# A deformable-convolution stage whose pairs are interpolated three turns ahead of their own, with the residual sums moved to the turn that ends a contraction

## The reference, cut to what matters

```python
x = x + layer0(gn(x))                       # batch 8, 256 channels, 64 x 64
    # qkv = w_qkv @ x; per head a 3x3 neighbourhood attention plus a 3x3 dynamic kernel; w_proj
x = x + modulated_dcn(gn(x), w_off, b_off, w)

def modulated_dcn(x, w_off, b_off, w):
    om = conv3x3(x, w_off) + b_off           # 27 channels: offsets y and x of 9 taps, 9 masks
    off, mask = om[:, :18], sigmoid(om[:, 18:27])
    py, px = base + tap + off                # a fractional place for each pixel and tap
    v = bilinear(x, py, px)                  # 4 neighbours, 4 weights
    return einsum('bckhw,ock->bohw', v * mask, w)
```

## Time and profile before

| | us |
|---|---|
| median of 3 runs | 5197.19 |
| lowest and highest run | 5186.94 and 5206.48 |
| the profiled execution | 5200.59 |
| its span (first to last instruction) | 5198.8 |
| TensorE busy | 4855.1 |
| VectorE busy | 4324.4 |
| ScalarE busy | 2332.2 |
| GpSimd busy | 2257.9 |

### The profile page before, as it was taken

How to read it: one execution, slowest core, us unless ns; L and a number is a source line. 1 busy time by engine, 2 the same in 40 slices (tenths; PEclk the granted TensorE clock), 3 DMA queues, 4 the chain that set the end, 5 groups by cost and what they waited for, 6 DMA issues and landing times. The chain is left out here.

```text
span 5198.8 us, 80271 instructions
## 1 busy us (share of the span) xinstructions
PE 4855.1 (93%) x26864; PEld 2671.2 (51%) x26864; DVE 4324.4 (83%) x11040; ACT 2332.2 (45%) x5584; POOL 2257.9 (43%) x2311
## 2 busy tenths in 40 slices
PE   7889999999999999999999999999999999988888
PEld 4545554555545555455545555455554555544444
DVE  6848888888888888888889888888888888987776
ACT  2244444344453444444444444434444344455555
POOL 0014444444444444444444444444444444455565
PEclk9999999999999999999999999999999999999999
DMA  5447878878787878978789787888878878798888
GB/s 180 143 153 263 284 260 321 284 270 278 274 325 269 275 272 281 339 252 282 266 274 339 261 278 266 288 315 270 281 267 310 290 263 275 258 356 313 328 324 305
DMA packets 490804, 1446.79 MB, mean 278 GB/s; under 512 B 47380, under 2 KB 117404, under 8 KB 490140
## 3 DMA queue, kind: packets, MB, share of 16 engines
q0 software_dynamic: 331776, 1208.11, 66.9%
q1 hardware_dynamic: 158620, 233.55, 12.6%
HBM read 1309.08 MB, written 132.39 MB: 277 GB/s over the span
## 5 line engine op out<-in xcount | busy, mean ns | idle before, releaser
L883 POOL DMA_INDIRECT G<-table,IDX x2304 | 2257.0, 980 | 2902.3 <-DVE V L1566 2094.9
L902 PE MATMUL ps<-VT,s_wconv 128*128 128x512 f32 x4608 | 2273.9, 617 | 102.0 <-ACT VT L1283 37.7
L1566 DVE SCALAR_TENSOR_TENSOR V<-G,WT,V 128x256 f32<-128x256 f32 x4320 | 1892.7, 479 | 115.8 <-DVE V L1566 3.7
L1283 ACT ACTIVATE VT<-ps 128x512 f32<-128x512 f32 x1152 | 686.7, 596 | 2294.5 <-PE ps L1122 1848.3
L902 PEld LDWEIGHTS ps<-VT,s_wconv 128*128 128x128 f32 x4608 | 823.7, 193 | 919.1 <-issue 847.0
L1553 DVE SCALAR_TENSOR_TENSOR V<-G,WT 128x256 f32<-128x256 f32 x2304 | 1009.0, 478 | 244.6 <-ACT G L1269 135.4
L1122 PEld LDWEIGHTS ps<-s_ident,V 128*128 128x128 f32 x4320 | 539.1, 142 | 650.4 <-issue 647.1
L1303 DVE TENSOR_TENSOR E<-ps,s_band 128x512 f32<-128x512 f32 x1024 | 648.7, 682 | 268.9 <-PE ps L964 137.3
L1269 ACT ACTIVATE G<-G,WT 128x256 f32<-128x256 f32 x1872 | 846.4, 498 | 16.1 <-DMA G<-table,IDX 12.3
L1122 PE MATMUL ps<-s_ident,V 128*128 128x128 f32 x4320 | 655.5, 275 | 47.6 <-DVE V L1566 43.0
L940 PE MATMUL ps<-XN,s_wqk 128*128 128x512 f32 x1024 | 488.5, 605 | 19.7 <-ACT XN L1182 16.7
(11 more groups left out here) (109 smaller groups left out, 3008.4 us busy)
## 6 DMA issues: line engine op xcount, KB each, us to landing
table<-E SPq DMA_DIRECT2D x256, 256.0 KB
G<-table,IDX POOLq DMA_INDIRECT x2304
X<-in_x SPq DMA_DIRECT2D x64, 512.0 KB
G<-in_x SPq DMA_DIRECT2D x56, 512.0 KB, 4.3
x<-X SPq DMA_DIRECT2D x56, 512.0 KB, 5.5
R<-x SPq DMA_DIRECT2D x56, 512.0 KB
out<-R SPq DMA_DIRECT2D x56, 512.0 KB
out<-X SPq DMA_DIRECT2D x8, 512.0 KB
```

What stands on the lines that cost most here:

```text
L883: e.indirect_dma_start(G[a % NG][:, :], None, T[b % 2], bass.IndirectOffsetOnAxis(ap=IDX[:, col:col + 1], axis=0)).then_inc(d_g[a % NG], 16)
L902: mm = e.matmul(CV[oh][:, :], s_wconv[:, h, t, oh * P:(oh + 1) * P], VT[U % 2][:, h, :], start=(t == 0 and h == 0), stop=(t == 8 and h == 1))
L1283: e.activation(VT[U % 2][:, :, 2 * P * pair:2 * P * (pair + 1)], BK[banks.place[use]][:, :].rearrange("p (h n) -> p h n", h=2), ACT.Copy). ...
L1566: e.scalar_tensor_tensor(vt[:, :], gt[:, q * C:(q + 1) * C], WT[:, col, q:q + 1], vt[:, :], ALU.mult, ALU.add).then_inc(lerp[q - 1], 1)
```

## The change

The loop that writes the steps is turned round. The lerps of pairs 0, 1 and 2 stand at the start of an image. From then on one round is: lerp m+2, two fills, turn m, the gather of pair m+5, scale m+4. So a lerp stands directly behind the turn whose transposes free its `V` buffers (m-1), and three turns ahead of its own. The two sums of a chunk each stand one turn earlier in the list, in the same step as the contraction that completes `CV`. Instructions, buffers and waits stay the same, but whether a pair is scaled on ScalarE or on VectorE is decided at the place where the scale step is written, which is now two pairs earlier: 203 pairs are scaled on VectorE in place of 216, and 949 on ScalarE in place of 936.

```diff
+        def interpolate(m):
+            if m < PAIRS:
+                steps.append(("lerp", b, m))
+
         steps.append(("gather", b, 0, NG))
         scale(0)
         scale(1)
         done = fill(0, done)
+        interpolate(0)
+        scale(2)
+        interpolate(1)
+        scale(3)
         for m in range(PAIRS):
-            steps.append(("lerp", b, m))
+            interpolate(m + 2)
             done = fill(2 * m + 1, done)
-            steps.append(("turn", b, m - 1))
-            if m > 0:
-                steps.append(("gather", b, 2 * (m - 1) + NG, 2 * m + NG))
-            scale(m + 2)
             done = fill(2 * m + 2, done)
-        steps.append(("turn", b, PAIRS - 1))
+            steps.append(("turn", b, m))
+            steps.append(("gather", b, 2 * m + NG, 2 * m + 2 + NG))
+            scale(m + 4)
         steps.append(("conv.end", b))
...
-                    if t == 1 and pair == 0 and u > 8:
+                    if t == 0 and pair == 1 and u > 8:
                         add_residual(b * NCH + c - 1, 0)
-                    elif t == 1 and pair == 1 and u > 8:
+                    elif t == 1 and pair == 0 and u > 8:
                         add_residual(b * NCH + c - 1, 1)
```

## The result

The changed kernel takes 5403.21 us (median of 4 runs, 5390.26 to 5407.31) against 5193.37 us for the kernel before (4 runs, 5186.94 to 5206.48): a ratio of 1.0396, 95% interval 1.0369 to 1.0424. The forecast of 5140 us, and the range up to 5225, are both wrong: the change makes the kernel slower by 4%.

What follows compares the result with a forecast made beforehand. TensorE, 93% busy, was taken as the bound, with VectorE close behind. From 5200.6 us: -33 lerps, -36 sums, -12 clock, -15 scales, +30 front work, +7 image starts gave 5141.6, written 5140 (ratio 0.989), range 5080 to 5225.

Steps and rivals of the forecast that it cites:

- What it costs: front work behind a lerp: Banded products queued on VectorE behind a lerp make TensorE wait for PSUM banks; +30 us, bounds 0 and 230.
- the slow rival: Half of 116 banded products have no slack, banks come free too late, low clocks follow; 5250 us, chance 0.18.
- an upper bound of 230 us: Added waits for banded products if none of the 116 places where VectorE was early had any slack.
- the slack at place 2: Near 586.76 us: TensorE wants the bank after 4.0 us, VectorE needs 3.3 for lerp and product; 0.7 us to spare.
- waits for ScalarE copies that grow by tens of microseconds: Sign in TensorE's waits, left alone in the sum, that would show the forecast wrong.
- Lerps, -33: Lerps three turns ahead cut the transposes' 43.0 us of waits for them to 10; bounds 0 and -43.
- 10.3 us of allowed lateness: How late VectorE may be at a turn with lerps three rounds ahead, up from 6.5 us.
- Residual sums, -36: Sums one turn earlier take 36 of 39.0 us from contractions' waits for them; bounds 0 and -39.
- the low clock at place 1, -12: Half-clock stretch from 786.7 to 790.1 us goes with the residual wait, 1.7 us in each of seven images.
- Scales and last image, -15: Scales two pairs earlier ease the last image's lerp, gather, scale loop that TensorE waits for; bounds 0 and -55.
- in the middle that gains TensorE nothing: Earlier scales spare VectorE waits for ScalarE, but in the middle gain TensorE nothing beyond the terms already counted.

Runs made afterwards that it cites:

- e17: Changed kernel with each of its two fills one quota step later, so turns stand behind the same front steps as in the kernel before; ratio 1.0231.
- e10: Kernel before with nine `G` buffers in place of ten and one place less for the statistics' loads; ratio 1.0013.
- e7: Kernel before with four `V` buffers in place of six, every instruction at its old place; ratio 1.0143.
- e13: Kernel before with only the fills half a round later against turns and lerps, lead and room of lerps kept at 1.5 rounds; ratio 1.0166.
- e1: Kernel before with the two residual sums alone moved one turn earlier; ratio 1.0033.
- e2: Changed kernel with the two residual sums back at their old turns; ratio 1.0457 to the kernel before.
- e3: Changed kernel with each lerp two turns ahead of its own instead of three; ratio 1.0169 to the kernel before.
- e4: Changed kernel with lerp m+2 between the two fills instead of ahead of both; ratio 1.0205 to the kernel before.
- e12: Kernel before for the first seven images, the whole change in the eighth alone; ratio 1.0002.
- e11: Kernel before with every scale written one pair earlier; ratio 1.0060.
- e6: Changed kernel with nine `G` buffers in place of ten and one place less for the statistics' loads; 5329.30 us, ratio 1.0518 to the kernel before.
- e5: Changed kernel with eight `V` buffers instead of six, nine `G` and one place less for statistics' loads; 5180.22 us, ratio 1.0225 to the kernel before.
- e9: Kernel before with eight `V` buffers in place of six, nine `G` and one place less for the statistics' loads; ratio 1.0011.

## Why the prediction was wrong, point by point

**The step that failed first: "What it costs: front work behind a lerp", +30 us.** The mechanism was named there and in the slow rival, and it is one that the runs show; its size was wrong. With the old place of the fills, TensorE's waits for banded products are 147 us in e17 against 54 in e10: +93 us of waits alone where I had +30. In the changed kernel, with the new place, they go from 58 to 192 us, +134. As a whole e17 costs 2.3%, which in the 5193 us of this kernel would be 120 us, net of what the rest of the change gains. I had worked out an upper bound of 230 us and then left it for a small value "because of the slack at place 2". That slack was a wrong sum. In the changed kernel place 2 reads:

```profile
591.61 0.60 PE L1128 MATMUL ps<-s_ident,V 128*128 128x128 f32 x4
...
592.28 1.27 DVE L1466 BATCH_NORM_STATS2 st<-X 128x6 f32<-128x512 f32 x2
593.47 0.86 DVE L1559 SCALAR_TENSOR_TENSOR V<-G,WT 128x256 f32<-128x256 f32 x2
...
596.77 0.66 PE L1128 MATMUL ps<-s_ident,V 128*128 128x128 f32 x4 [0.79 <-DVE E L1309]
```

I had let VectorE begin the lerp at the turn; it begins 1.3 us after the turn's end, behind the sum and the statistics of the projection (L1339 and L1466), which the instruction order of place 2 shows directly ahead of it. So the 3.3 us of VectorE work became more than TensorE's 4.0, and instead of 0.7 us to spare there is a wait of 0.79. The second error was to let only waits into the term, no clock: low-clock time is 154 us in e17 against 122 in e10, and 355 us against 182 in the changed kernel. In the slow rival I had some 34 us for it; TensorE's busy time for the same work grew by 72. The clock does not follow every kind of wait, though: in e7 TensorE is idle for 307 us and its low-clock time is 119 us, no more than in e10.

**The step that was missing: the place of the fills.** The sum has no term for it. The diff turns `fill, turn m-1, fill` into `fill, fill, turn m`, and I read this as the same two fills in a round. It moves each turn half a round against the front, costs 1.7% (e13) or 86 us by itself, with lead and room of the lerps as they were. The forecast's last paragraph named its sign in the trace, waits for ScalarE copies that grow by tens of microseconds: `KP` went from 18.3 to 39.9 us and `XN` from 16.7 to 39.5. I could have looked for it: the order of ScalarE's list at those waits was to be had before the run.

**Lerps, -33.** Right as far as the wait goes: 17.1 us are left, 10 were forecast (8 us in e17, by the records). "10.3 us of allowed lateness" left out that VectorE pays for it elsewhere, in its waits for the turn.

**Residual sums, -36, and the low clock at place 1, -12.** The wait went as forecast, from 39.0 to 1.7 us. Alone it is worth nothing (e1: 1.0033); inside the new order it is worth 0.6% (e2 against the changed kernel), about the size forecast. The -12 failed: in all seven images a wait for a banded product took the place of the residual wait, and the low clock stayed. The Trainium skill, TensorE: Matmul & The Clock Gate, "A second HAM failure mode: psum-queue depth-cycling", warned of micro-idles between groups of matmuls; the trace agrees in direction, with 475 us of idle TensorE and 355 us of low clock against 340 and 182; e7, with more idle time and no more low clock than e10, shows that it is not enough to know the idle time.

**Scales and last image, -15.** The last image became 18 us shorter (from 474 to 456 us from its first turn to the end), and VectorE's waits for scaled neighbours vanished (0.6 us in the whole trace). But e2, e3 and e4, at the same level and with scales as early, have last images of 469, 476 and 469 us, so that the scales gave the 18 us is not shown. In the later batches the last image takes some 404 us already in the old order (e10), and the same edit there gains nothing (e12). That the term came out near its size may be luck. And "in the middle that gains TensorE nothing" overlooked a loss, the 0.6% of e11.

**The rivals.** "Slower, by banks that come free too late" was the right one, with 0.18 and 5250 us; its price lacked the place of the fills, and the range, which ended at 5225, cut it off. Even with the upper bound of 230 us for the waits the sum would have been 5342 us, 61 us short; the missing step is of that order (86 us).

## What to carry to other kernels

Where an engine works through a fixed list, count for each producer two distances, not one: how far ahead of its consumer it stands, and how far behind the step that frees its buffer. Moving it ahead takes from the second what it gives to the first; here 1.5 rounds of each were enough, and room 0 instead of one round cost 2.8% (e6 against e5), while the extra lead gave 26 us less waiting at the turns. When a loop is written in another order, count also where the work woven into it falls against the steps that it hides: half a round here cost 1.7%, with the buffers, the room and practically all instructions as before. When you price a new wait at a place, count everything that stands ahead of the late instruction in its engine's list, not only the piece that moved.

## What the runs showed that I had not expected

The same program does not see the same clock in each image. In e1 the first images take from 623.3 to 637.8 us, with 10 to 31 us of low-clock time in each; in e9, in another batch, six images take 616.9 to 618.5 us with 7 to 14 us. The kernel before takes 5193 and 5210 us in the first two measurements and 5063 to 5065 us in the four others, and 70 us of this lie in the last image (474 us, against 404 us in e10). In that stage more is moved in the same time as well: 330 GB/s from 4780 to 5140 us in the kernel before, 395 GB/s from 4720 to 5020 us in e10, which has the same order. The record gives the first and the third batch the same chip number, and they lie at different levels, so the number does not tell them apart; what does is not shown. A gain that rests on idle time in one stage of one measurement, as mine in the last image did, may not be there in the next.
